# Moving one small gather per tile from the SyncE queue to the ScalarE queue in an attention and mixture-of-experts kernel

## The reference, cut to what matters

```python
router_logits = xt @ gate_w.T
routing_weights = softmax(router_logits)
top_w, top_idx = top_k(routing_weights, 8)
full_w = normalised(top_w at top_idx, 0 elsewhere)      # 2048 x 32
g = silu(einsum('th,ehi->eti', xt, w_gate))             # h = 512, i = 192
u = einsum('th,ehi->eti', xt, w_up)
y = einsum('eti,eih->eth', g * u, w_down)
out = einsum('eth,te->th', y, full_w)                   # added to x
```

## Time and profile before

| what | value |
| --- | --- |
| median of 3 runs | 831.02 us (830.6 to 839.17) |
| span of the profiled execution | 758.7 us |
| what of the median lies outside the span | 72.3 us |
| busy share PE, PEld, DVE, ACT, POOL | 93, 77, 75, 57, 50% |
| granted TensorE clock, mean over the span | 0.984 |
| xw transfers on SP's queue | 145 |

### The profile page before, as it was taken

How to read it: one execution, slowest core, us unless ns; L and a number is a source line. 1 busy time by engine, 2 the same in 40 slices (tenths; PEclk the granted TensorE clock), 3 DMA queues, 4 the chain that set the end, 5 groups by cost and what they waited for, 6 DMA issues and landing times.

```text
span 758.7 us, 24265 instructions
## 1 busy us (share of the span) xinstructions
PE 708.8 (93%) x3682; PEld 584.4 (77%) x3683; DVE 566.7 (75%) x1355; ACT 434.8 (57%) x1047; POOL 380.1 (50%) x297
## 2 busy tenths in 40 slices
PE   7999999988788799999999999999999999999994
PEld 5466555656667688889988999889988889888993
DVE  4578888878655488677877878877887778767882
ACT  1775666662035366556666666666667566656662
POOL 2006777767776434443544544434553455444554
PEclk9999999999799999999999999999999999999997
DMA  8996777587898999999999999999999999999995
GB/s 297 361 335 234 261 269 288 215 289 273 291 299 188 184 211 224 218 202 237 215 225 240 225 211 238 224 251 228 244 236 245 211 229 248 243 210 227 220 155 79
DMA packets 174405, 179.85 MB, mean 237 GB/s; under 512 B 36864, under 2 KB 128768, under 8 KB 174368
## 3 DMA queue, kind: packets, MB, share of 16 engines
q0 software_dynamic: 30976, 73.48, 43.0%
q1 hardware_dynamic: 118240, 67.67, 35.1%
q10 hardware_dynamic: 25152, 38.30, 15.6%
HBM read 92.25 MB, written 87.13 MB: 236 GB/s over the span
## 4 chain that ended last, share of the span: by engine, by line
SPq 38%; PE 23%; issue 18%; DMA 7%; POOL 7%; ACT 4%; DVE 2%; ACTq 1%; DVEq 1%; POOLq 0%
SPq L320 23%; SPq L325 8%; POOL x_sorted L512 6%; SPq L439 5%; PE bank L1532 3%; PE bank L1533 3%; PE bank L1539 3%; DMA x_sorted<-xn_kept,slots 3%; DMA x_all<-x_sorted 2%; PE bank L1325 2%; DMA x_sorted<-prob,last_slots 1%; PE bank L1504 1%; ACT prob L670 1%; PE bank L1505 1%; PE bank L1506 1%
## 5 line engine op out<-in xcount | busy, mean ns | idle before, releaser
L569 POOL DMA_INDIRECT out_dram<-ctx_all,x_all x144 | 243.2, 1689 | 276.7 <-issue 131.5
L1532 PE MATMUL bank<-gu_hi,xT_hi 128*128 x576 | 194.7, 338 | 2.1 <-ACT xT_hi L800 1.2
L1533 PE MATMUL bank<-gu_lo,xT_hi 128*128 x576 | 195.6, 340 | 0.0
L813 ACT ACTIVATE ctx_all<-bank 128x512 f32<-128x512 f32 x144 | 86.0, 597 | 104.9 <-issue 78.9
L512 POOL DMA_INDIRECT x_sorted<-xn_kept,slots x96 | 100.0, 1042 | 86.7 <-issue 82.0
L1539 PE MATMUL bank<-gu_hi,xT_lo 128*128 x576 | 137.9, 361 | 0.0
L1208 DVE STREAM_TRANSPOSE x_all<-x_all 128x512 f32<-128x512 f32 x146 | 103.9, 712 | 26.5 <-DMA x_all<-x_sorted 22.2
L1255 DVE SCALAR_TENSOR_TENSOR probT<-probT,x_all,bank 128x192 f32<-128x192 f32 x144 | 59.5, 413 | 79.3 <-ACT probT L821 70.5
L1532 PEld LDWEIGHTS bank<-gu_hi,xT_hi 128*128 128x128 f32 x576 | 108.5, 188 | 10.7 <-issue 5.0
L1533 PEld LDWEIGHTS bank<-gu_lo,xT_hi 128*128 128x128 f32 x576 | 108.4, 188 | 5.6
L800 ACT ACTIVATE xT_hi<-x_all 128x512 fp32r<-128x512 f32 x146 | 91.7, 628 | 34.7 <-DVE x_all L1208 34.6
(11 more groups left out here) (222 smaller groups left out, 1109.7 us busy)
## 6 DMA issues: line engine op xcount, KB each, us to landing
x_all<-x_sorted SPq DMA_DIRECT2D x578, 64.0 KB
gu_raw<-in_w_gate_up_dram ACTq DMA_DIRECT2D x28, 768.0 KB
down_raw<-in_w_down_dram ACTq DMA_DIRECT2D x28, 512.0 KB
x_sorted<-pad_rows SPq DMA_DIRECT2D x1, 8720.0 KB, 31.3
x_all<-in_x_dram SPq DMA_DIRECT2D x8, 512.0 KB, 4.9
ctx_all<-in_ctx_dram SPq DMA_DIRECT2D x8, 512.0 KB, 6.6
out_dram<-x_all SPq DMA_DIRECT2D x8, 512.0 KB, 5.9
gu_raw<-in_w_gate_up_dram SPq DMA_DIRECT2D x4, 768.0 KB
```

The lines of the kernel that those rows point to most:

```text
L569: pool.indirect_dma_start(out=out, out_offset=bass.IndirectOffsetOnAxis(ap=xw[:, k, E:E + 1].bitcast(I32), axis=0), in_=y_sb[:, i, :], in_ ...
L813: act_e.activation(y_sb[:, i, :], bank[6 + i % 2][:], ACT.Copy).then_inc(S["y_evac"], 1)
L1532: pe.matmul(out_gu, xT_hi[:, s, c * P:(c + 1) * P], gate_up(gu_hi, c), start=(c == 0), stop=False)
L1533: pe.matmul(out_gu, xT_hi[:, s, c * P:(c + 1) * P], gate_up(gu_lo, c), start=False, stop=False)
```

## The change

From tile 10 on, SP issues only the four DMAs of x. ACT issues the DMA of xw, three tiles ahead: at the end of its program of tile j it reads the row of tile j+3 from the table and issues the transfer. Before its first one it waits once for the last scatters. xw has four semaphores of its own, `xw_loaded[i]`; `xg_loaded` now counts four DMAs a tile where it counted five. DVE waits for `xw_loaded` ahead of its wait for `sil_ready`. The first ten tiles keep their order of issue.

```diff
-    LOADS, BLOCKS = HC + 1, 16
+    LOADS, BLOCKS = HC, 16
+    XW_BY_SP, XW_AHEAD = SLOTS + 2, 3
...
-            eng.dma_start(xw[...], rows[:, H:RW]).then_inc(xg_loaded[i], 16)
+            eng.dma_start(xw[...], rows[:, H:RW]).then_inc(xw_loaded[i], 16)
...
                 load_x_part(sp, rows, i, range(HC))
-                block = k % BLOCKS if type(eight) is int else SLOTS * sp.snap(...) + k % SLOTS
-                load_xw(sp, rows, i, block)
+                if not is_before(eight, k, XW_BY_SP):
+                    return
+                load_xw(sp, rows, i, k)
...
+            def load_coming_xw(q, k):
+
+                if tile_is_before(q, k, XW_BY_SP - XW_AHEAD):
+                    return
+                if tile_is_before(q, k, XW_BY_SP - XW_AHEAD + 1):
+                    for c in range(TOPK):
+                        act_e.wait_ge(last_scattered[c], column_count(c))
+                act_e.reg_load(row_reg, x_row[0:1, bass.ds(4 * q + k + XW_AHEAD, 1)])
+                rows = x_sorted[bass.ds(act_e.snap(row_reg, min_val=0, max_val=SPARE), P), :]
+                n, i = divmod(k + XW_AHEAD, 4)
+                block = 4 * ((q + n) % 4) if type(q) is int else 4 * act_e.snap((q + n) & 3, min_val=0, max_val=3)
+                load_xw(act_e, rows, i, block + i)
...
                     evac_y(j - 2, (k - 2) % 4, None if tile_is_before(q, k, 6) else 16 * (q + (k - 6) // 4 + 1))
+                load_coming_xw(q, k)
...
+                dve.wait_ge(xw_loaded[k], 16 * q + 16)
                 dve.wait_ge(S["sil_ready"], j + 1)
```

More of the change, by code:

```diff
@@ L231, in build @@
         xg_loaded = [sem(f"xg_loaded{i}") for i in range(4)]
+        xw_loaded = [sem(f"xw_loaded{i}") for i in range(4)]
         last_scattered = [sem(f"last_scattered{k}") for k in range(TOPK)]
@@ L323, in load_xw @@
         def load_xw(eng, rows, i, block):
-            eng.dma_start(xw[:, bass.ds(block, 1), :].rearrange("p a w -> p (a w)"), rows[:, H:RW]).then_inc(xg_loaded[i], 16)
+            eng.dma_start(xw[:, bass.ds(block, 1), :].rearrange("p a w -> p (a w)"), rows[:, H:RW]).then_inc(xw_loaded[i], 16)
         def early_row(eng, k, passed, row_reg, code_reg, column_reg, need_reg):
@@ L456, in load_tile @@
                 load_x_part(sp, rows, i, range(HC))
-                block = k % BLOCKS if type(eight) is int else SLOTS * sp.snap((eight + k // SLOTS) & 1, min_val=0, max_val=1) + k % SLOTS
-                load_xw(sp, rows, i, block)
+                if not is_before(eight, k, XW_BY_SP):
+                    return
+                load_xw(sp, rows, i, k)
             sp.wait_ge(last_scattered[TOPK - 1], column_count(TOPK - 1))
@@ L846, in _ @@
             act_e.wait_ge(S["down_raw_loaded"], 16 * E)
+            wait_apart(act_e, "act_passed", *((xw_loaded[i], 16 * turns + 16 * (i < XW_AHEAD)) for i in range(4)))
         @block.vector
```

## The result

The change makes the kernel slower: 912.8 us, median of 4 runs (909.45 to 917.56), against 831.99 (830.6 to 839.17), a ratio of 1.095 (95% interval 1.089 to 1.101), or 81 us. Timed again later, the same pair gave 846.2 against 758.6, a ratio of 1.113 (1.105 to 1.121), or 88 us.

A forecast was written before the change was run, and what follows sets the result against it. PE bounds the kernel before at 3.65 us a tile, ACT's sequencer the changed one at 3.05 + 1.0 = 4.05; 134 x 0.40 = 54 us, so 831.0 + 54 = 885 us, range 852 to 918.

The forecast's parts named there:

- The bound: Tile loop before: PE sets the pace at 3.65 us a tile; ACT needs about 3.10, with 0.55 to spare.
- the larger figure: ACT's spare time in the tile loop if waits before L813 count too: 0.73 us a tile, 97.2 us.
- The added cost of 1.0 us: ACT's table read, xw issue and register work between L813 and the next silu: 1.0 us a tile, lower bound 0.81.
- the 3.05 of the forecast: ACT's own need in the tile loop before the added work: 3.05 us a tile.
- The sum, 54 us: Tile loop: ACT's need of 4.05 us a tile against 3.65, over 134 tiles, adds 54 us.
- The profiled span, 72.3 us shorter: Whole program: the profiled span, 72.3 us shorter than the median before, should be about 813 us after the change.
- SP's relief: SP's loop tile falls from 3.25 to about 2.6 us without xw; by itself wins between nothing and 20 us.
- The late silu's way to PE: Through DVE's product: about 1.9 us of lateness is free; PE's idle time before L1506 grows to 40 to 60 us.
- Hidden cost: Rival: ACT's added time falls where it waits anyway, SP is relieved; 812 us at best; chance of faster 0.08.
- Transfers as the bound: Rival: the 16 DMA engines set the pace, so moving the request changes nothing, 827 to 839 us; chance 0.05.
- Late xw: Rival: xw lands behind weights on ACT's queue and DVE waits; 56 us, 887 with ACT hidden; chance 0.04.

The follow-up runs named there:

- issue only: Kernel before, with ACT also issuing a 16.5 KB DMA each tile to a place nobody reads, SP keeping xw: 855.21 us, ratio 1.005.
- copy unread: Kernel before, SP keeping xw; ACT also reads the row and issues a copy of xw to a place nobody reads: 831.35 us, ratio 1.094.
- second issue: Changed kernel, with ACT also issuing a 16.5 KB DMA each tile to a place nobody reads: 900.3 us, kernel before on that chip 761.32.
- the GpSimd runs: Changed kernel, but GpSimd issues xw, five tiles ahead: behind its add 894.66 us, ratio 1.051; ahead of its add 843.63 us, ratio 1.108.

## Why the prediction was right, and where it was off

**The bound.** Right: PE set the pace before, and ACT has little to spare. The stretch gives 3.10 us a tile as ACT's need, with 0.55 us to spare; "issue only" then added an issue of 0.38 us at no cost, and the runs together put the room at 0.34 to 0.40 us of sequencer records a tile, gaps left out, which is nearer to the 0.55 than to the 0.73 of the larger figure. The page's 57% would have allowed three times as much.

**The added cost of 1.0 us.** Right in kind, too small in size. The read was costed at its median, 0.287 us; its records have the same median and a long tail, and their mean is 0.413. The lines of the read and of the issue on ACT's sequencer, as in the earlier trace rows:

```profile
L825 ACTq TENSOR_LOAD <-x_row x137: 215/288/1028, 313.3 to 894.7; - x137
```

```profile
L327 ACTq DMA_DIRECT2D x_all<-x_sorted x138: 348/358/407, 251.9 to 895.3; - x138
```

The tail was in sight, at 1153 ns for the maximum in the earlier trace rows. With the means: 0.41 for the read, 0.36 for the issue and 0.37 for the register work and gaps between them make 1.15 us, from the start of the read to the end of the issue. In that stretch of code the trace has three register instructions in half of the tiles and five in the others, and one more ahead of the read; the prediction counted three in all. With the 3.05 of the forecast that is 4.20 us a tile, against 4.28 measured.

**The sum, 54 us.** The stretch grew by 84 us, the total by 81. Of the 30 us that were missing in the stretch, 134 x 0.15 = 20 are the mis-sized cost, most of it the tail of the read. Another 12 are waits that the forecast took as used up: ACT still waited 11.4 us for PE and 0.3 for DVE. The rest of ACT's tile is then (573.2 - 11.7) / 134 - 1.15 = 3.04 us, near the 3.05 that was chosen between 2.93 and 3.10. That this fits so closely is in part luck, since some register work lies outside the 1.15 us, and how much of the added work a running instruction covers isn't known. 912.8 lies near the upper end of the range because of these two.

**"The profiled span, 72.3 us shorter".** Wrong, and so is the table ahead of the prediction, which puts these 72.3 us outside the span. The span of one execution was held against the median of others. In every later run the span lies about 2 us below the time of its own execution, and the experiments saw medians of 758.6 and 761.3 us for this kernel. It did no harm, since the sum used the difference and not the span, but 813 was forecast for the span and 909.1 measured.

**SP's relief.** Right for SP itself: its own time fell from 3.4 to 2.7 us a tile, by the 0.7 us that was forecast, and its waits are 190.1 us where the copy, with xw left on SP, shows 62.5. DVE's wait for x fell from 22.2 us to this:

```profile
  DMA x_all<-x_sorted: 7.2, 5
```

But that is no sign of the relief, since it fell as far (8.8 us) in the copy: a slower loop leaves SP time to catch up. What the relief might have won is hidden behind ACT.

**The late silu's way to PE.** Right in kind, too large in size. PE's idle time before its L1506, put down to DVE's product, is this, where 13.9 stood before:

```profile
PE bank L1506 <- DVE probT L1274: 30.1, 60, 2.0
```

I said 40 to 60. PE's weight loads for the same line waited 58.9 us for that product; how the slower tile shows in the other matmuls wasn't taken apart.

**The rivals.** Hidden cost: excluded. "Issue only" shows how near it was: an issue alone would have been hidden, but whether SP's relief would then have won time was not run. Transfers as the bound: excluded, the share fell and the loop grew. Late xw: no wait for a DMA at three tiles of lead. The Trainium skill's half sentence, in "DMA: Bandwidth & Descriptors", section "Issuing engines are not separate DMA queues", that the time to start a DMA is "usually small relative to the DMA itself", does not tell what decides here. What counted was the start against the spare time of the engine that issues: an issue of 0.38 us alone was covered, and an issue with its read and registers, 1.15 us together, cost 84 us over 134 tiles. With its other half, that starting DMAs from several engines saves sequencer time only, "copy unread" and "second issue" agree: there ACT's loop follows the sequencer's time.

## What to carry to other kernels

Ask of an engine not how busy it is but how long it stands ready and waits for another; idle time that is put down to "issue" may be its sequencer at work, and then it can't be filled. Look at the sequencer's records before you say so: they covered 148 of 160 us for ACT after the change, and 25 of 176 for POOL in one of the GpSimd runs. Here ACT, with a busy share of 57%, had room for about 0.4 us of sequencer time a tile: one DMA issue fitted, an issue with its table read did not, and from there each microsecond of sequencer time cost about a microsecond of the loop. And cost an instruction that is repeated in a chain by the mean of its records, not by the median, when its maximum is several times the median.

## What the runs showed that was not expected

**The first part differs by 95 us between executions of one kernel.** The same program took 212.7 us to the end of the first tile's gate/up product in one profile and 308.2 in another; the changed kernel took 285.4 and 216.6. The windows of the first part, of the first profile and of the repeated kernel before:

```profile
0.00:212.70 212.70, 192.21 (x959) 122.05 (x961) 160.38 (x545) 106.07 (x237) 119.97 (x138) 0.98 0.80 284
```

```profile
0.00:308.20 308.20, 223.80 (x953) 143.04 (x962) 162.35 (x546) 107.33 (x238) 132.43 (x149) 0.82 0.60 209
```

The busy times of DVE and ACT are nearly the same, and PE's granted clock is 0.82 in the mean instead of 0.98. The second profile has pauses of PE that are put down to issue, 14 before the weight loads of its filler matmuls, where the first has 4 of 1.8 us together:

```profile
PEld bank L1300 <- issue: 28.4, 14, 4.7
```

The loop after it takes the same time in both, 531.1 and 529.3. The medians of the kernel before are 758.6 and 761.3 us on two chips, 850.9 on a third, and 832.0 in the first pair; they go with the length of the first part, which was 213 to 217 us in all profiles of the first two chips and 302 to 308 on the third. What makes the pauses is open. It is the reason to compare a kernel with the kernel before on the same chip, or stage by stage.

**Reads of a table from SBUF have a tail.** ACT's reads of L760 take 0.27 us at the least, 0.29 in the median and up to 1.15 us, and SP's up to 1.0 in the same trace. L760 averages 0.39 us over the loop of the kernel before; over the loops of the other runs the averages of ACT's read lines lie between 0.30 and 0.43 us.
